# A fused gather, mixing and dequantizing matmul kernel: load order, first output piece and two residual steps rearranged

## The reference

```python
def reference(x, itok, cond_weights, qweight, scale, zero_point, bias):
    W = cond_weights[itok]                          # x: (64, 64, 1024), W: (64, 64, 64)
    y = jnp.einsum('bct,bcd->bdt', x, W)            # mixing of the 64 channels
    w = (unpack_6_bit(qweight) - zero_point) * scale   # (1024, 1024), from 1024 x 768 int32
    return x + jnp.einsum('bsk,nk->bsn', y, w) + bias
```

## Time and profile before

| | |
|---|---|
| Time before, median of 3 runs | 288.01 us (287.66 to 294.14) |
| The profiled execution: its own time | 287.66 us |
| Its span in the profile | 285.4 us |
| Granted TensorE clock, mean | 1.00 of full speed |
| PE busy | 279.1 us, 98% of the span |
| DVE / POOL / ACT busy | 188.6 / 94.5 / 83.3 us |
| Chain that ended last | PE 92%, DVE 4%, DMA 1% |

### The profile page before, as it was taken

How to read it: one execution, slowest core, us unless ns; L and a number is a source line. 1 busy time by engine, 2 the same in 40 slices (tenths; PEclk the granted TensorE clock), 3 DMA queues, 4 the chain that set the end, 5 groups by cost and what they waited for, 6 DMA issues and landing times.

```text
span 285.4 us, 8520 instructions
## 1 busy us (share of the span) xinstructions
PE 279.1 (98%) x3323; PEld 233.2 (82%) x3323; DVE 188.6 (66%) x254; ACT 83.3 (29%) x170; POOL 94.5 (33%) x38
## 2 busy tenths in 40 slices
PE   7999999899999999999999999999999999999995
PEld 3988888788888888888888888888888888888885
DVE  3685999855567666865559555676667655595554
ACT  3677412531045300732017310453006320050000
POOL 0009563234440444304443344404443044430000
PEclk9999999999999999999999999999999999999999
DMA  7982463544124521445115541145214451101112
GB/s 276 401 301 80 160 226 112 193 156 155 73 83 161 200 96 69 147 157 190 73 73 181 163 152 73 73 162 198 99 73 148 157 191 73 73 37 73 73 73 73
DMA packets 20685, 39.48 MB, mean 138 GB/s; under 512 B 6850, under 2 KB 7106, under 8 KB 20674
## 3 DMA queue, kind: packets, MB, share of 16 engines
q1 hardware_dynamic: 19730, 36.96, 36.6%
q10 hardware_dynamic: 944, 2.38, 2.3%
HBM read 22.54 MB, written 16.78 MB: 138 GB/s over the span
## 4 chain that ended last, share of the span: by engine, by line
PE 92%; DVE 4%; DMA 1%; issue 1%; ACTq 1%; ACT 0%; DVEq 0%
PE o_ps L281 78%; PE y_ps L250 8%; PE y_ps L281 2%; DVE resid L505 2%; PE o_ps L250 2%; DMA q_raw<-in_L_ffn_qweight_dram 1%; PE o_ps L292 1%; PE y_ps L263 1%; PE o_ps L263 0%; DVE o_sb L514 0%; DVE o_sb L522 0%; ACT L433 0%; ACTq L140 0%; DVE y_lo L495 0%; PE y_ps L292 0%
## 5 line engine op out<-in xcount | busy, mean ns | idle before, releaser
L281 PE MATMUL o_ps<-qT,y_hi 128*128 128x512 f32 (+2 forms) x520 | 197.9, 385 | 0.0
L281 PE MATMUL o_ps<-qT,y_lo 128*128 128x512 f32 (+2 forms) x520 | 196.7, 382 | 0.0
L614 POOL TENSOR_TENSOR resid<-x_sb,bias_bc 128x1024 f32<-128x1024 f32 x32 | 93.8, 2934 | 157.3 <-DVE o_sb L522 136.9
L281 PEld LDWEIGHTS o_ps<-qT,y_hi 128*128 128x128 f32 x520 | 97.1, 188 | 19.5 <-ACT qT L427 0.2
L281 PEld LDWEIGHTS o_ps<-qT,y_lo 128*128 128x128 f32 x520 | 97.2, 188 | 18.9
L514 DVE TENSOR_TENSOR o_sb<-o_ps,scale_bc 128x512 f32<-128x512 f32 x61 | 42.2, 692 | 76.5 <-PE o_ps L281 76.0
L522 DVE TENSOR_TENSOR o_sb<-o_sb,resid 128x512 f32<-128x512 f32 x63 | 51.3, 818 | 2.1
L402 ACT ACTIVATE junk<-x_sb 128x1024 bf16<-128x1024 f32 x32 | 33.8, 1058 | 54.1 <-DMA x_sb<-in_x_dram 54.1
L505 DVE SCALAR_TENSOR_TENSOR resid<-zs_bc,ysum,resid 128x1024 f32<-128x1024 f32 x32 | 46.0, 1438 | 0.0
L495 DVE TENSOR_TENSOR y_lo<-y_ps,y_hi 128x512 fp32r<-128x512 f32 x57 | 35.1, 683 | 5.7 <-ACT y_hi L411 5.7
L420 ACT ACTIVATE ysum<-y_ps 64x2 f32<-64x2 f32 x18 | 3.0, 165 | 106.5 <-PE y_ps L292 98.0
(11 more groups left out here) (34 smaller groups left out, 58.7 us busy)
## 6 DMA issues: line engine op xcount, KB each, us to landing
x_sb<-in_x_dram SPq DMA_DIRECT2D x32, 512.0 KB, 3.3
out_dram<-o_sb SPq DMA_DIRECT2D x63, 256.0 KB, 2.1
q_raw<-in_L_ffn_qweight_dram ACTq DMA_DIRECT2D x6, 384.0 KB, 5.4
w_sb<-in_L_cond_weights_dram SPq DMA_DIRECT2D x63, 16.0 KB, 1.9
q_raw<-in_L_ffn_qweight_dram SPq DMA_DIRECT2D x2, 384.0 KB, 6.8
scale_bc<-_L_ffn_weight_scale_dram SPq DMA_DIRECT2D x1, 512.0 KB, 5.1
zs_bc<-n_weight_zero_point_dram SPq DMA_DIRECT2D x1, 512.0 KB, 5.7
bias_bc<-in_L_ffn_bias_dram SPq DMA_DIRECT2D x1, 512.0 KB, 6.5
```

What stands on the lines that cost most here:

```text
L281: last = nc.tensor.matmul(bank, part[:, slot, kt, :], qT[:, kt, col:col + width], start=(kt == 0 and part is y_hi), stop=(kt == KT - 1 and ...
L614: nc.gpsimd.tensor_tensor(resid[:, j % RING, :], x_sb[:, j % RING, :], bias_bc[:], ALU.add).then_inc(xbias_ready, 1)
```

## The change

Four edits are made in the opening, none in the loop trips apart from the way in which SP picks weights.

1. ACT's queue issues block 0 of `qweight`, then its half of tile 0's weights, then blocks 1 to 5. Before, blocks 0 and 1 stood ahead of the weights, and 2, 3, 5, 7 behind. SP's queue issues blocks 6 and 7 where it issued 4 and 6. SP also issues each half of a tile's weights directly behind its own register load (in all tiles), in place of both loads first.
2. PE makes the first piece of tile 0 as one of 256 columns, 16 matmuls, in place of two of 128 columns, 32 matmuls; so it waits for two placed blocks where it waited for one. One of two filling matmuls (`keep_warm`) behind the first transposes goes.
3. ACT places block 3 ahead of the row sum of tile 0.
4. DVE computes the residuals of tiles 2 and 3 ahead of the additions of tiles 1 and 2, in place of behind them.

```diff
@@ -160,9 +160,8 @@
 
             def load_w(j, i):
                 t = i * RING + j
-                picked = [pick(sp, t * 2 + half) for half in range(2)]
                 for half in range(2):
-                    load_w_half(sp, j % RING, half, picked[half])
+                    load_w_half(sp, j % RING, half, pick(sp, t * 2 + half))
 
             def reload(j, i):
 
@@ -195,7 +194,7 @@
             load_w_half(sp, 0, 0, pick(sp, 0))
             load_x(1, 0)
             load_w(1, 0)
-            for n in (4, 6):
+            for n in (6, 7):
                 load_q(sp, n)
             for j in range(2, RING):
                 load_x(j, 0)
@@ -341,18 +340,16 @@
             keep_warm(WARMUP)
             pe.wait_ge(ident_ready, 1)
             transpose_q(0)
-            keep_warm(2)
+            keep_warm(1)
             wait_mix(0, 0)
             mix(0, y_banks[0])
             transpose_q(1)
             transpose_q(2)
-            pe.wait_ge(qt_ready, 1)
+            pe.wait_ge(qt_ready, 2)
             pe.wait_ge(y_hi_ready, 2)
-            products(o_ps[:, 0, 0:P], 0, P, 0, parts=(y_hi,))
+            products(o_ps[:, 0, 0:2 * P], 0, 2 * P, 0, parts=(y_hi,))
             wait_linear(0, 0, 0)
-            products(o_ps[:, 0, 0:P], 0, P, 0, parts=(y_lo,))
-            pe.wait_ge(qt_ready, 2)
-            products(o_ps[:, 0, P:2 * P], P, P, 0).then_inc(o_ps_ready[0], 1)
+            products(o_ps[:, 0, 0:2 * P], 0, 2 * P, 0, parts=(y_lo,)).then_inc(o_ps_ready[0], 1)
             transpose_q(3)
             wait_mix(1, 0)
             mix(1, y_banks[1])
@@ -427,20 +424,19 @@
                 nc.scalar.activation(qT[:, :, n * P:(n + 1) * P], qt_banks[n % 2].bitcast(I16), ACT.Copy,
                                      bias=-QCENTER).then_inc(qt_ready, 1)
 
-            for n in range(2):
-                load_q(act, n)
+            load_q(act, 0)
             act.wait_ge(warm_ready, 1)
             nc.scalar.activation(junk[:, 1, 0:1], warm[:, 0:1], ACT.Copy)
             act.wait_ge(ids_loaded, 16)
             load_w_half(act, 0, 1, pick(act, 1))
-            for n in (2, 3, 5, 7):
+            for n in range(1, 6):
                 load_q(act, n)
             place_q(0)
             high(0, 0, y_banks[0])
             place_q(1)
             place_q(2)
+            place_q(3)
             sum_x(0, 0)
-            place_q(3)
             high(1, 0, y_banks[1])
             sum_x(1, 0)
             place_q(4)
@@ -560,15 +556,14 @@
                 add_residual(0, 0, h)
             residual(1, 0)
             scale_out(2, 0, 0)
+            residual(2, 0)
             for h in range(H):
                 add_residual(1, 0, h)
             scale_out(2, 0, 1)
-            residual(2, 0)
+            residual(3, 0)
             for h in range(H):
                 add_residual(2, 0, h)
-            scale_out(3, 0, 0)
-            residual(3, 0)
-            add_residual(3, 0, 0)
+            finish(3, 0, 0)
             finish(3, 0, 1)
 
             with dve.Fori(1, TRIPS - 1) as i:

```

## The result

The changed kernel takes 289.57 us (median of 15 runs, 287.95 to 290.78) against 287.77 us (15 runs beside them): a ratio of 1.0062, 95% interval 1.0043 to 1.0081. It is slower, by 0.6%, where I said 0.1% faster, and it spreads over 2.8 us. Its runs fall into two sets by the mean granted clock of the run: six at 0.998 to 1.000 take 287.95 to 288.90 us, nine at 0.992 to 0.994 take 289.43 to 290.78. The medians of the two sets are 288.57 and 290.21, 1.6 us apart. The kernel before loses clock now and then too: one of its 33 runs in one set beside the experiments and one of 29 in another had 0.994 (289.52 and 289.76 us).

The account below looks back on a forecast made before the run. PE bounds the kernel, gated in the first trip by DVE's `y_lo`; the residual order gains 0.40 us, the opening's edits 0. Profiled 287.66 - 0.40 = 287.3, median 0.35 above: 287.6 us, range 286.6 to 288.7.

Parts of the forecast that it names:

- Block 1 ... should land at 6.1 to 6.6, no later than PE can use it: Opening loads: block 1, with 384 KB less ahead of it than block 2 had, lands at 6.1 to 6.6 us.
- block 2 at 8.5, at most 9.0: Opening loads: block 2, issued behind tile 1's x, lands at 8.5 us, bounded by 7.7 and 9.0.
- With the same bytes ahead: Opening loads: tile 1's x landed at 9.0 us behind the same bytes, which bounds block 2's landing.
- Rival 4: Opening: PE's new gap, about 1.3 us more, costs granted clock; products take about 2 us longer, 289.3 us; chance 0.03.
- 1.00 throughout, gaps included: PE's granted clock in the trace before was 1.00 even in gaps, set against a loss of clock.
- A saving on PE in the opening alone buys nothing: First trip's fourth mix: DVE's `y_lo` comes 0.60 us after PE's own arrival, so the opening's PE edits are worth 0.
- might go too: First trip's fourth mix: up to 0.5 us more gain if its pause goes, within a rival of chance 0.18.
- DVE's and POOL's turns: First trip: DVE and POOL alternate whole instructions; residuals ahead of additions bring DVE's gate from 50.31 to 49.91, gaining 0.40 us.
- The piece: Opening on PE: one piece of 256 columns in place of two of 128 saves 1.4 us of PE.
- ACT's row sum: Opening on ACT: tile 0's row sum ahead of tile 1's copies starts them 2.75 us behind the fourth transposes, formerly 1.76.
- The picks: SP's queue: the same register loads and DMAs in another order are worth 0; nothing waits there.
- turns between queues: Opening loads: DMA engines alternate queues by packet, so block 2 lands near 8.0 us; the sum stays the same.

Follow-up runs that it names:

- three filling matmuls: Changed kernel with the earlier load order, both ACT row sums behind tile 1's copies and three filling matmuls behind the third transposes, against the kernel before: 288.38 us, ratio 1.0017.
- the filled one: Changed kernel plus six filling matmuls ahead of the second and six ahead of the third transposes, against the kernel before: 288.47 us, ratio 1.0025.
- loads undone: Changed kernel with the load order of before, its other edits kept, against the kernel before: 287.50 us, ratio 0.9985.
- the x moved ahead: Changed kernel with tile 1's x issued on SP ahead of the wait for the ids, against the kernel before: 289.55 us, ratio 1.0069.

## Why the prediction was wrong, by its steps

**The step that failed first: "Block 1 ... should land at 6.1 to 6.6, no later than PE can use it", and block 2 at 8.5, at most 9.0.** In the changed kernel they were unpacked at 7.90 and 10.15, in its second profile at 7.16 and 9.43. I bounded a load by the bytes ahead of it, as if the DMA engines stayed full. But the loads ahead, block 0 and one x, had been moved by about 4.5 us (from 4.5 to 5.0 the engines moved 34 GB/s in the first profile, 143 in the second, 365 before), and the next issue of a block, at 4.1 or 3.5, hung on the ids and on a register load; from that issue to block 1's unpacking took 3.7 to 3.8 us in both profiles. "With the same bytes ahead" is no bound where nothing is queued. The upper end of 9.0 was wrong for the same reason.

**Rival 4, the clock, had 0.03 and is about half of the loss** (1.1 of 1.8 us in one set of runs, 0.5 of 1.2 in the other). Its mechanism and its price were right: it had about 2 us, of which 0.2 to 0.6 hidden, and a run that loses clock is 1.6 to 1.7 us slower. Its chance was wrong, and that its total of 289.3 lies near the 289.57 measured is luck: it leaves out the late blocks (0.8) and has every run lose clock. I took "1.00 throughout, gaps included" as evidence, but the longest gap inside PE's work in that trace is 0.6 us, while I had myself named one 1.3 longer. Filling the gaps took the loss of clock away and brought the spread from 2.8 to 1.7 us.

**"A saving on PE in the opening alone buys nothing": wrong.** I named DVE's `y_lo` as the last gate of the first trip. The gate behind it is PE's own: an instruction transfer that starts about 2 us behind the first mix. The view of DMAs, for the 0.1 us in which it starts (packets, MB, share of 16 engines' window), 48.6 to 48.7 in the kernel before:

```profile
q8 instruction: 1, 0.02, 76.2%
```

and 51.4 to 51.5 in the changed one:

```profile
q8 instruction: 1, 0.02, 102.6%
```

That is 0.762 x 16 x 0.1 = 1.22 us of transfer to 49.9, and 1.64 to 53.1; PE went on at 51.14 and 54.42, 1.3 behind each end. In the 14 profiles of this case the transfer begins 1.7 to 2.8 us behind the start of the mixes, takes 0.9 to 1.9, and PE resumes 1.1 to 1.4 behind its end, whether it had waited for `y_lo` (0.3 to 0.6) or not. So the wait that I wanted to shorten lay inside another that mostly moves with PE. I had the 0.50 us pause before me and left it out of the sum as something that "might go too".

The traces show one thing more: the pause has a fixed place in PE's program. In 13 of the 14 profiles it stands behind exactly 721 recorded matmuls of PE, in the 14th (three filling matmuls) behind 720, and some records can be missing. In the mixes' 256 small matmuls that is behind the 198th in the four kernels without the whole piece, behind the 203rd in the filled one, behind the 215th in eight of the nine others, whose program is 17 matmuls shorter ahead of it, and behind the 212th in the one with three filling matmuls more. Behind the mixes all 14 profiles take the same time to the end, 233.19 to 233.25 us. A wait for another engine or for data would not follow the count of matmuls so; this speaks for PE waiting for its own instructions. That the transfer seen is the one it waits for is still inferred; I ran nothing that removes it.

**What was right.** DVE's and POOL's turns: 0.40 forecast, 0.41 measured. The piece: 1.4 us of PE forecast, 1.6 measured (2.02 from first product to fourth transposes, 3.61 before); it started 0.77 later, mostly for the second placed block (0.70), so that the fourth transposes came 0.8 earlier where it stood alone. ACT's row sum: copies of tile 1 forecast 2.75 behind the fourth transposes, 2.63 measured (17.77 less 15.14), so that with loads undone the first wide matmul is at 17.32, where the piece alone has it by 16.87 and the kernel before at 17.41. In the times of those two (0.9985 and 0.9983) this difference is not resolved. The picks: nothing. The rule of the Trainium skill's page "DMA: Bandwidth & Descriptors", section "Queues, rings and completion order", on turns between queues could not be judged here, since the queues were empty first; block 2, which I had landing near 8.0 by it, was unpacked at 10.15 and 9.43.

**The sum with the measured terms**, for the first set of runs: +0.7 for late blocks, +1.1 for the clock, less nothing for the rest: 287.77 + 1.8 = 289.6. The 1.1 is what the other term leaves over, so that the sum is no check; for it speaks that nine of 15 runs lost clock at 1.6 us each, 1.0 in the mean.

## What to carry to other kernels

Before a load is moved behind a wait, look at what is queued in front: a DMA queue that is fed by an engine which waits for another DMA can run dry, and then the order of bytes says nothing. Where an edit opens a gap on PE that is longer than any in the trace, "full clock throughout" is no evidence for it: put half a clock behind it into the sum, with a chance that isn't small, and look at the clock of every run and not only of the profiled one. A wait that is followed by a pause "for nothing" may be hiding it: shorten the one, and the other grows.

## What the runs showed that I had not expected

- A float32 matmul of 128 columns costs PE as much as one of 256: 0.11 us against 0.12 apart, 3.58 for 32 against 2.17 for 16.
- PE fell from full to half clock behind two idle stretches of 1.6 us with 0.6 us of work between (10 to 14 us above), and behind one of 1.60 with the x moved ahead. Pauses of 1.59 and 1.71 us in the fourth mix (filled, and three filling matmuls) did not cost it, with a mean of 1.000 in both profiles. Nor did a gap of 1.61 in the opening itself (8.9 to 10.53, with one of 0.56 ahead of it) in the profile of the load order alone, where the clock is 1.00 from 10 to 16 us, though four of that kernel's six runs lost clock: a gap's length alone doesn't tell, and the same program loses clock in one execution and not in another.
- PE pauses 0.5 to 1.7 us at one fixed place of its program, and goes on 1.1 to 1.4 us behind the end of a 16 KB instruction transfer, once, in its first pass through the loop; in later trips the same mixes run through. 17 matmuls fewer ahead of that place moved the pause 17 matmuls further into the mixes, and that alone gave 0.3 us.
